# A two-layer graph network on one core: the last unit worked tile by tile, smaller first loads, and part of the last inner norm on ScalarE and GpSimd

## The reference, cut to what matters

```python
# block 1: masked attention over the graph, 12 heads of 32
q, k, v = x @ Wq + bq, x @ Wk + bk, x @ Wv + bv
s = q k^T / sqrt(32) + beta * adj;  s = where(adj > 0, s, -9e15)
h = layernorm(x + softmax(s) @ v)                       # eps 1e-5, no gain or bias
# block 2: two inner layers l = 0, 1 on z = h
for l in range(2):
    a = softmax(z z^T / sqrt(384)) * adj
    a = a / (rowsum(a) + 1e-10)
    c = (a * upper) @ (z @ Wl[l].T + bl[l]) + diag(a) * (z @ Ws[l].T + bs[l]) \
        + (a * lower) @ (z @ Wr[l].T + br[l])
    z = relu(norm(c, 1e-12) * g[l] + b[l])              # the inner norm, with gain and bias
out = layernorm(h + z)                                  # eps 1e-5
```

## Time and profile before

| | |
|---|---|
| runs | 1292.51, 1292.63, 1294.82 us |
| profiled execution | 1295.08 us, of which the span from the first to the last instruction is 1293.4 us |
| TensorE | busy 1261.8 us (98%), granted clock 0.990 in the mean |
| VectorE, ScalarE, GpSimd | busy 984.8, 629.7 and 366.7 us |

### The profile page before, as it was taken

The page is one execution under the profiler, slowest core; times in us unless marked ns, Lnnn a source line. Parts: engine busy times, 40 slices in busy tenths (PEclk is TensorE's granted clock), DMA queues, the critical chain, the costliest instruction groups (busy, mean ns, idle before and its releaser), DMA issues.

```text
span 1293.4 us, 34503 instructions
## 1 busy us (share of the span) xinstructions
PE 1261.8 (98%) x13844; PEld 1168.9 (90%) x13844; DVE 984.8 (76%) x2672; ACT 629.7 (49%) x1329; POOL 366.7 (28%) x398
## 2 busy tenths in 40 slices
PE   8999999999999999999999999999999999999885
PEld 8999999999999999999999999999999999999774
DVE  5777778777778777878777878777878777787765
ACT  5544554544554544554534554445545445545432
POOL 3222323322323232323222323222323222323211
PEclk9999999999999999999999999999999999999997
DMA  8211111011110111110111110111110111110000
GB/s 273 82 40 57 57 57 30 29 56 57 57 57 24 35 56 57 57 57 18 41 57 56 57 57 7 51 57 57 57 49 9 57 57 57 57 35 12 26 13 25
DMA packets 52206, 66.32 MB, mean 51 GB/s; under 512 B 17744, under 2 KB 38352, under 8 KB 51920
## 3 DMA queue, kind: packets, MB, share of 16 engines
q1 hardware_dynamic: 52048, 64.12, 16.3%
HBM read 38.54 MB, written 12.58 MB: 40 GB/s over the span
## 4 chain that ended last, share of the span: by engine, by line
PE 96%; DVE 2%; issue 1%; ACT 1%; POOL 0%; DMA 0%; POOLq 0%; ACTq 0%; SPq 0%; DVEq 0%
PE bank L359 25%; PE bank L361 23%; PE bank L360 23%; PE bank L550 7%; PE bank L462 4%; PE bank L499 4%; PE bank L447 3%; PE bank L428 3%; PE bank L475 2%; PE bank L485 2%; PE bank L530 1%; DMA late<-in_w_qk 0%; DVE ln_six L1012 0%; DVE probs L900 0%; POOL probs L1184 0%
## 5 line engine op out<-in xcount | busy, mean ns | idle before, releaser
L359 PE MATMUL bank<-w_hi,hT_hi 128*128 128x384 f32 x1158 | 405.2, 350 | 1.9 <-DVE hlr L966 1.0
L361 PE MATMUL bank<-w_hi,hT_lo 128*128 128x384 f32 x1158 | 390.3, 337 | 0.0
L360 PE MATMUL bank<-w_lo,hT_hi 128*128 128x384 f32 x1158 | 390.1, 337 | 0.0
L359 PEld LDWEIGHTS bank<-w_hi,hT_hi 128*128 128x128 f32 x1158 | 218.4, 189 | 6.6 <-issue 2.2
L360 PEld LDWEIGHTS bank<-w_lo,hT_hi 128*128 128x128 f32 x1158 | 219.0, 189 | 0.0
L361 PEld LDWEIGHTS bank<-w_hi,hT_lo 128*128 128x128 f32 x1158 | 218.5, 189 | 0.0
L966 DVE TENSOR_TENSOR hlr<-bank,rows 128x384 f32<-128x384 f32 x256 | 142.0, 556 | 79.4 <-PE bank L361 76.6
L1197 POOL TENSOR_TENSOR ln_rstd<-ln_var,minus_half 128x2 f32<-128x2 f32 x128 | 98.7, 771 | 350.6 <-DVE ln_var L1018 131.5
L1184 POOL TENSOR_TENSOR probs<-probs,row_max 128x768 f32<-128x768 f32 x64 | 94.3, 1475 | 275.9 <-DVE row_max L906 275.9
L981 DVE TENSOR_TENSOR late<-bank,rows 128x384 f32<-128x384 f32 x128 | 71.3, 557 | 123.5 <-PE bank L361 123.5
L359 PE MATMUL bank<-xT_hi,w_hi 128*128 128x256 f32 x558 | 158.8, 285 | 0.0
(11 more groups left out here) (101 smaller groups left out, 2349.0 us busy)
## 6 DMA issues: line engine op xcount, KB each, us to landing
v_halves<-v_stage SPq DMA_DIRECT2D x128, 99.0 KB, 2.3
xT_in<-in_xT SPq DMA_DIRECT2D x32, 384.0 KB, 3.5
x_in<-in_x SPq DMA_DIRECT2D x32, 384.0 KB, 4.1
out<-late SPq DMA_DIRECT2D x32, 384.0 KB, 2.4
late<-in_w SPq DMA_DIRECT2D x7, 576.0 KB, 5.7
adj_in<-in_adj SPq DMA_DIRECT2D x32, 96.0 KB, 3.9
adjT_in<-in_adjT SPq DMA_DIRECT2D x64, 48.0 KB, 3.2
rows<-in_vectors SPq DMA_DIRECT2D x1, 1536.0 KB, 8.0
```

Source lines behind the costliest of these rows:

```text
L359: nc.tensor.matmul(o, l_hi, r_hi, start=first and n == 0, stop=False)
L360: nc.tensor.matmul(o, l_hi, r_lo, start=False, stop=False)
L361: done = nc.tensor.matmul(o, l_lo, r_hi, start=False, stop=final and n == last)
```

## The change

**Start.** x of unit 0 comes in three DMAs (one for each chunk), the q and k weights in six of 192 KB; ScalarE issues the first of them itself, SyncE the others. The splits on ScalarE and VectorE are per piece. The k of chunk 2 has a bank of its own, so that ScalarE can take q while k is computed. ScalarE splits the v weight after it has taken chunk 1.

**Step 0.** ScalarE does `exp_gram(0)` first, then the splits of weights 6 and 7, `split_x`, the split of 8. VectorE does the split of 6 after the bias of tile 0's right side, of 7 after that of tile 1's left side, and so after the score masks; it waits for the bias rows' DMA, and for all weights' low parts ahead of the first `self_bias_tile`.

**All steps.** `h0` has three slots, the context of layer 1 two (`c1[unit % 2]`), and `y_stored` is a pair of semaphores. The order of middle steps is as before.

**Step 30** (`next_to_last`): TensorE does the probabilities' transposes and `attend` right after `mix(0)`, and `transpose_z` behind them; `transpose_h` moves ahead of tile 1's right side product, and both self products stand before `mix(1)`. VectorE masks three of four score banks first and takes the maxima early.

**Units 29 and 30, inner norm of layer 1**: ScalarE normalizes (`final_normalize`), GpSimd multiplies by g and adds b (`final_weight`, `final_bias`), VectorE keeps relu and sum (`final_add`).

**Step 31** (`last`): each tile has its own mix, statistics, inverse root, shift, normalization, transposes, gram, maximum, exponential and mask, with other PSUM banks; the chunks of z are taken and split one at a time (`last_take_z`, `last_low`), and layer 1's left product begins on chunk 0 with the gram in between. FINAL of unit 31 is inside this step, on VectorE as before but tile by tile, and each tile is stored by itself. Step 32 is empty but for those two stores.

```diff
+            def next_to_last(st):                      # TensorE, step 30
+                gram(st, 0)
+                project_sides(st, 0)
+                transpose_e(st, 0)
+                project_self(st, 0, 0)
+                project_self(st, 0, 1)
+                mix(st, 0)
+                transpose_probs(st)
+                attend(st)
+                transpose_z(st)
+                gram(st, 1)
+                project_side(st, 1, 0, LEFT)
+                project_side(st, 1, 0, RIGHT)
+                project_side(st, 1, 1, LEFT)
+                transpose_h(st)
+                project_side(st, 1, 1, RIGHT)
+                transpose_e(st, 1)
+                project_self(st, 1, 0)
+                project_self(st, 1, 1)
+                mix(st, 1)
...
+            def last_left_and_gram(st, t):
...
+                for kc in range(KC):
+                    need(pe, z_hi, KC * t + kc + 1)
+                    need(pe, z_lo, KC * t + kc + 1)
+                    done = product(LAST_HLR_BANKS[1][2 * t + LEFT][:, 0:D],
+                                   [((hT_hi[:, t, kc, :], hT_lo[:, t, kc, :]), weight(W_LATE + 3 + LEFT, kc))],
+                                   first=kc == 0, final=kc == KC - 1)
+                    if kc == 0:
+                        last_gram(st, t)
+                done.then_inc(hlr_psum, 1)
...
+            def last(st):                              # TensorE, step 31
+                gram(st, 0)
+                last_side(st, 0, 0, LEFT)
+                last_side(st, 0, 0, RIGHT)
+                transpose_e(st, 0)
+                last_self(st, 0, 0)
+                last_mix(st, 0, 0)
+                last_side(st, 0, 1, LEFT)
+                last_side(st, 0, 1, RIGHT)
+                last_self(st, 0, 1)
+                last_transpose_z(st, 0)
+                last_mix(st, 0, 1)
+                last_left_and_gram(st, 0)
+                last_side(st, 1, 0, RIGHT)
+                last_transpose_e(st, 0)
+                last_self(st, 1, 0)
+                last_transpose_z(st, 1)
+                last_mix(st, 1, 0)
+                last_left_and_gram(st, 1)
+                last_side(st, 1, 1, RIGHT)
+                last_transpose_e(st, 1)
+                last_self(st, 1, 1)
+                last_mix(st, 1, 1)
...
+            def final_normalize(st):                   # ScalarE, units 29 and 30
...
+                for t in range(T):
+                    nc.scalar.activation(c[:, t], c[:, t], ACT.Identity, bias=ln3_shift[:, t:t + 1],
+                                         scale=ln3_rstd[:, t:t + 1]).then_inc(f_normal, 1)
...
+                for kc in range(KC):                   # ScalarE, last_take_z
+                    nc.scalar.activation(hT[:, t, kc, :], LAST_Z_BANKS[t][:, kc * P:(kc + 1) * P], ACT.Relu,
+                                         bias=b0_col[:, kc:kc + 1], scale=g0_col[:, kc:kc + 1]).then_inc(z_taken, 1)
+                    act.wait_ge(z_taken, KC * t + kc + 1)
+                    nc.scalar.activation(hT_hi[:, t, kc, :], hT[:, t, kc, :], ACT.Copy).then_inc(z_hi, 1)
...
+            def last(st):                              # ScalarE, step 31
+                exp_gram(st, 0)
+                final_normalize(st)
+                scale_self(st, 0)
+                last_z(st, 0)
+                last_take_z(st, 0)
+                scale_turned(st, 0)
+                last_exp(st, 0)
+                last_z(st, 1)
+                last_take_z(st, 1)
+                scale_self(st, 1)
+                last_exp(st, 1)
+                normalize_final(st)
+                scale_turned(st, 1)
+                last_normalize(st, 0)
+                last_normalize(st, 1)
...
+            def last(st):                              # VectorE, step 31
...
+                shift(st, FINAL, ln3_mv, ln3_rstd, ln3_shift, ln3_rs, ln3_sh)
+                self_bias_tile(st, 0, 0)
+                need(dve, dz_ready, st.count(LATE, 2, 1))
+                make_ctx_first(st, LATE, 0)
+                last_z_stats(st, 0)
+                sides_bias(st, 0, 1, LEFT)
+                last_shift(st, 0, ln1_mv, ln1_rstd, ln1_shift, z_rs, z_sh)
+                final_add(st, 0)
+                sides_bias(st, 0, 1, RIGHT)
+                final_add(st, 1)
+                self_bias_tile(st, 0, 1)
+                last_low(st, 0)
+                last_max(st, 0)
+                make_ctx_second(st, LATE, 0)
+                last_z_stats(st, 1)
...
+                last_mask_aT(st, 1)
+                self_bias_tile(st, 1, 1)
+                final_add(end, 0)
+                last_sum_stats(end, 0)
+                dve.wait_ge(tile_dz, 2)
+                make_ctx_second(st, LATE, 1)
+                last_end_stats(st, 1)
+                final_center(end, 1)
+                last_shift(end, 0, ln2_mv, ln2_rstd, ln2_shift, y_rs, y_sh)
+                final_scale(end, 1)
+                final_add(end, 1)
+                last_sum_stats(end, 1)
+                last_shift(end, 1, ln2_mv, ln2_rstd, ln2_shift, y_rs, y_sh)
...
+            def last(st):                              # GpSimd, step 31
+                inverse_root(st, FINAL, 1, 1, ln3_eps, ln3_var, ln3_rstd, ln3_rs)
+                final_weight(st, 0)
+                final_bias(st, 0)
+                final_weight(st, 1)
+                last_inverse_root(0, z_eps, ln1_var, ln1_rstd, z_rs)
+                final_bias(st, 1)
+                last_inverse_root(1, z_eps, ln1_var, ln1_rstd, z_rs)
+                inverse_root(st, FINAL, 1, 1, ln2_eps, ln2_var, ln2_rstd, ln2_rs)
...
-            sp.dma_start(xT_in[:, 0], xT[0]).then_inc(xT_loaded[0], 16)
+            for kc in range(KC):
+                sp.dma_start(xT_in[:, 0, kc], xT[0, :, kc]).then_inc(x0_in[kc] if kc < KC - 1 else xT_loaded[0], 16)
...
+            act.dma_start(qk_raw[:, 0, 0], w_qk[0, :, 0]).then_inc(qk_raw_in[0][0], 16)
```

More of the change, by code:

```diff
@@ L246, in qk_bank, with k_psum @@
             return FIRST_QK_BANKS[unit][m] if unit < 2 else QK_BANKS[m]
+        def k_psum(unit, m):
+            if unit == 0 and m == KC - 1:
+                return bank[6][:, 0:TOK]
+            return qk_bank(unit, m)[:, TOK:2 * TOK]
         def h_bank(unit, t):
@@ L342, in step @@
                     load_x(st, MID + 1)
-                if st.has(FINAL):
+                if st.has(FINAL) and st.unit(FINAL) == LAST:
+                    for t in range(T):
+                        need(sp, y_ready, st.count(FINAL, 2, t + 1))
+                        sp.dma_start(out[LAST][:, t], context(LAST, 1)[:, t]).then_inc(y_stored[LAST % 2], 16)
+                elif st.has(FINAL):
                     need(sp, y_ready, st.count(FINAL, 2, 2))
-                    sp.dma_start(out[st.unit(FINAL)], c1).then_inc(y_stored, 16)
+                    sp.dma_start(out[st.unit(FINAL)], context(st.unit(FINAL), 1)).then_inc(y_stored[st.slot(FINAL)], 16)
                 if st.has(EARLY):
@@ L349, in _ @@
             steps(step)
-            sp.wait_ge(y_stored, 16 * UNITS)
+            for i in range(2):
+                sp.wait_ge(y_stored[i], 8 * UNITS + (16 if i == LAST % 2 else 0))
         @block.tensor
@@ new lines, in last_gram @@
+            def last_gram(st, t):
+                need(pe, z_taken, KC * t + KC)
+                if t == 0:
+                    need(pe, hlr_ready, st.count(LATE, 8, 3))
+                for kc in range(KC):
+                    for g in range(GRAPHS):
+                        a = hT[:, t, kc, g * N:(g + 1) * N]
+                        done = nc.tensor.matmul(LAST_TILE_BANKS[t][g * N:(g + 1) * N, 0:N], a, a,
+                                                start=kc == 0, stop=kc == KC - 1)
+                done.then_inc(tile_u, 1)
@@ new lines, in final_normalize, with last_z @@
+            def final_normalize(st):
+                c = context(st.unit(FINAL), 1)
+                act.wait_ge(ln3_sh, st.unit(FINAL) - (UNITS - 3) + 1)
+                for t in range(T):
+                    nc.scalar.activation(c[:, t], c[:, t], ACT.Identity, bias=ln3_shift[:, t:t + 1],
+                                         scale=ln3_rstd[:, t:t + 1]).then_inc(f_normal, 1)
+            def last_z(st, t):
+                act.wait_ge(z_sh, t + 1)
+                nc.scalar.activation(c0[:, t], c0[:, t], ACT.Identity, bias=ln1_shift[:, t:t + 1],
+                                     scale=ln1_rstd[:, t:t + 1]).then_inc(z_ready, 1)
@@ L784, in step @@
                     return
-                if early:
-                    split_x(st)
-                if late:
+                if st.unit(MID) == UNITS - 1:
+                    next_to_last(st)
+                    return
+                if st.unit(LATE) == LAST:
+                    last(st)
+                    return
+                if st.unit(FINAL) == LAST:
+                    return
+                if late and st.unit(LATE) == 0:
+                    exp_gram(st, 0)
+                    split_weight(6)
```

(8 more changed lines are left out.)

556 lines of the change are left out of this document (456 added, 100 removed).

## The result

The changed kernel takes 1282.79 us (median of 4 runs, 1282.44 to 1282.98), the kernel before beside it 1292.64: ratio 0.992, 95% interval 0.9902 to 0.9937. It is faster by 9.85 us, where 15.9 were forecast: 1282.79 us lies outside the forecast's own 1273 to 1279 and 0.2 us inside the wide range of 1272.5 to 1283.0. The profiled execution took 1282.61 us, with a span of 1280.9.

What follows compares the result with a forecast made beforehand. TensorE, busy 98% of the span, bounds the kernel, so only the ends can move. Gains of 1.2 + 1.0 + 0 + 3.6 + 7.3 + 2.8 = 15.9 us give 1276.7 us; own range 1273 to 1279, 8-in-10 range 1272.5 to 1283.0.

Steps and rivals of the forecast that it cites:

- Step 31 and tail: Last unit tile by tile: step 31 gains 7.3 us up to the last mix, the tail behind it 2.8 us.
- Step 30: Transposes and attend fill TensorE's wait for z at full clock; the step gains 3.6 us, bounds 1.3 and 4.0.
- The price of the half clock: TensorE's slow clock after its waits for z costs some 2.6 us in step 30, 3.7 us in step 31.
- Rival (a): The clock falls in step 30 again, costing 2.6 us: 1279.3 us; chance 0.15.
- Step 0: Weight splits moved behind tile 0's biases end TensorE's 0.98 us wait: gain 1.0 us, bounds 0.2 and 1.0.
- The opening: Smaller loads and piecewise splits before the scores bring them 1.2 us earlier; bounds nothing and 1.9 us.
- rival (c): The opening and step 0 give nothing, losing 2.2 us: 1278.9 us; chance 0.06 alone.
- The middle steps: Same order on all engines, no new TensorE wait: zero gain, bounds -0.5 and +1 us over 28 steps.
- The last subtraction: Gains found in the 1295.08 us profiled execution are subtracted from the 1292.63 us median: 15.9 off gives 1276.7 us.

Runs made afterwards that it cites:

- the repeat: The changed kernel itself, unedited, measured again in a follow-up group beside the kernel before: 1282.95 us, ratio 0.9914.
- warm30: Changed kernel with six spare matmuls around the transposes of z in step 30 to keep TensorE's clock: 1282.01 us.
- best2: Changed kernel with GpSimd's step 0 split of x held back, spare matmuls in step 30, and GpSimd's first-norm root ahead of gain and bias: 1280.04 us.
- before_warm2: Kernel before with 22 spare matmuls ahead of the transposes of z in steps 30 and 31, 2 and 5 behind: 1292.43 us.
- before_warm: Kernel before with 12 spare matmuls ahead of the transposes of z in steps 30 and 31, 2 behind in step 31: 1292.59 us.
- mix_tile: Kernel before with each mix's matmuls issued tile by tile instead of left for both tiles, then right: 1294.55 us, one run.
- mix_split: Kernel before with each mix issued tile by tile and one small full-array matmul between the tiles: 1405.82 us, one run.
- pool0: Changed kernel with GpSimd's low part of x in step 0 held until VectorE has split weights 6 and 7: 1281.38 us.

## Why the prediction was only half right

*Step 31 and tail: right in sum, in step 31 by luck.* Forecast 7.3 + 2.8 = 10.1 us; 6.6 + 3.7 by the profiles, and 9.5 to 10.4 by undoing it. Inside step 31 both terms were off and nearly cancelled: TensorE was busy 29.31 us instead of 25.0, of which the tile-wise mixes are 3.0 us (the other 1.3 I can't place), and it waited 0.4 us instead of 4.0. The mechanism held: the chains fit behind the other tile's products, better than I had laid them out. The tail gained 0.9 us more than forecast.

*Step 30: the step that failed.* Forecast 3.6, measured 1.15 us (0.7 in the repeat). The sentence "the probabilities' transposes and attend now run in the wait, at full clock" held, and z came at the forecast time: 1224.0, where 1225.0 less the 1.1 us by which this step starts earlier is 1223.9. Three things behind it didn't. The clock fell although TensorE stood no longer than 2.0 us at a time; I had written that it would be busy only 1.5 of 5.1 us there, but argued from the longest empty stretch. Gain and bias on GpSimd double VectorE's low parts. And with the clock held the first norm is next, 0.8 us (0.79 in warm30), which is the same contention again: VectorE's variance was late, not GpSimd's root. I had put GpSimd's four new instructions into GpSimd's queue and at nothing on VectorE. best2, which takes away all three, gives back 2.0 of the 2.45 us missed.

*The price of the half clock: mis-sized.* I took it from TensorE's work alone, 2.6 and 3.7 us. Rival (a) came true as an event and not in its price: 0.7 to 1.1 us in step 30 of the changed kernel, and in the kernel before 1.4 and at least 0.7. The busy time that a full clock saves counts only as far as no other chain ends just after it.

*Step 0: 0.1 instead of 1.0 us, from a wait that is not always there.* Two things went wrong. I had said that the mask of aT "fits by one instruction", with 1.3 us for each split; beside GpSimd one took 2.96. The rule that I cited for step 31 from the Trainium skill (SBUF — State Buffer, Who interferes with whom), two SBUF inputs of VectorE against GpSimd's reads, applied here, and the trace agrees: 2.96 against 1.34 us. I had not asked it where the change moved a split beside GpSimd's `split_x`.

And the 0.98 us that I wanted to win are not a fixed cost of the kernel before. In its other executions (of kernels whose text is the same up to this place) TensorE's wait is 0.91 us in before_warm2, but 0.17 in before_warm, 0.21 in mix_tile and 0.16 in mix_split. The profile before, then before_warm:

```profile
41.01 0.60 POOL L1171 TENSOR_TENSOR adj_diag<-adj_in,diag_sel 128x192 f32<-128x192 f32 x1
41.02 0.74 DVE L953 TENSOR_TENSOR diag_junk<-e_di,adj_diag 128x128 f32<-128x128 f32 x1
```

```profile
40.28 0.28 DVE L961 TENSOR_TENSOR diag_junk<-e_di,adj_diag 128x128 f32<-128x128 f32 x1
40.32 0.70 POOL L1179 TENSOR_TENSOR adj_diag<-adj_in,diag_sel 128x192 f32<-128x192 f32 x1
...
41.69 0.41 PE L359 MATMUL bank<-w_hi,hT_hi 128*128 128x384 f32 x1 [0.17 <-DVE hlr L974]
```

Where GpSimd's instruction starts just ahead of VectorE's, VectorE's takes 0.74 us instead of 0.28, and the bias behind it is late. Step 0 of the kernel before lasts 40.25, 39.44, 40.18 and 39.52 us in four executions, that of the changed kernel 40.16 to 40.19 in every one without pool0's edit: against the mean of the former it is 0.3 us longer, and even pool0's 39.36 is only 0.1 below the good ones.

*The opening: nothing.* 1.2 forecast, 0.54 between the two profiles, and less over more executions: unit 0's first `gram` starts at 34.67, 34.32, 33.94, 33.95 and 33.80 us with the opening of before, mean 34.14, and at 34.13, 33.83, 34.06, 34.89, 33.70, 34.20 and 33.66 with the new one, mean 34.07. Spread, not gain. The first product is earlier in every execution (5.55 to 5.88 us where the old opening has 6.53 to 6.86), and the scores wait 0.56 to 0.79 us for their take instead of 0.93, so the edits did their part; the scores start at 13.82 to 14.64 us before and at 13.61 to 14.90 after, so something between them, which no run here isolates, takes it back. The sum had a slip too: 7.90 less 7.2 is 0.7 us, where I took 0.9. Opening and step 0 together are rival (c), which I gave 0.06 alone.

*The middle steps: right*, 0.45 us better, within the spread: from unit 0's `gram` to step 30's the executions of both kernels and of those built on them, mixes kept together, take 1171.5 to 1172.7 us, step 0 included.

*The last subtraction.* The profiled execution of the kernel before was 2.45 us above the median of its first runs, that after 0.2 below. I took gains found in that trace off the median whole, although that execution was longer than the mean over all that I have, by 0.5 us in the opening and 0.4 in step 0. Part of the difference is the median itself: the first four runs gave 1292.64 us, the 43 later ones medians of 1293.4 to 1294.3. Trace and median differ by 2.65 of the 6.05 us missed; beyond what is named here, no trace shows where it lies.

*The range.* What came was (a) and (c) together with that difference; the range had been laid to hold one rival at a time. That it still holds the time, by 0.2 us, is luck: the tail gave 0.9 us more than forecast, the clock's price was smaller than in (a), and the errors within step 31 cancelled.

## What to carry to other kernels

Work out a faster clock or a removed wait as the distance to the chain that ends next, not as the time removed: 2.6 us of slow clock were worth 0.7 to 1.4 here, since another engine's queue ended just behind. Before an instruction is moved, look at what VectorE or GpSimd does beside it at the new place and at what is queued behind it on the engine that follows; both undid edits here that were right by themselves. Look for a wait in several executions before its length goes into a sum: the 0.98 us of step 0 were 0.16 to 0.21 in three others. Splitting the last unit by tile pays when the other tile's products cover each chain, even with 3 us of worse packing.

## What was unexpected of the hardware

- TensorE ran the 64x64 matmuls of a mix four at a time in both orders of issue tried, with work for all four quarters close by (1.54 us for sixteen records, tile by tile); with a full-array matmul between the tiles it is 1.51 us each.
- The same kernel text in step 30 ran at clock 0.53 and 0.59 (over 7 us) in two executions; with another opening alone it ran at 1.00, with waits of 2.0 and 1.4 us as in the second of them. Whether the clock falls in this step is a chance, which one trace doesn't show.
- The contention costs either engine: of two equal GpSimd instructions for `adj_side` in step 0 the one beside VectorE's split took 1.69 us and the other 0.52, and that split kept its 1.34; the split before it took 2.96 instead.
